# A graph network on one core: the second convolution's sums as four 32-column products side by side on TensorE, and 84 gathered groups in place of 100

## The reference

```python
def _gcn_conv(x, src, dst, norm, W, b, n_nodes):
    h = x @ W
    msg = h[src] * norm[:, None]
    out = jax.ops.segment_sum(msg, dst, num_segments=n_nodes)
    return out + b
...
h = jax.nn.relu(_gcn_conv(x, src, dst, norm, W1, b1, n))
h = jax.nn.relu(_gcn_conv(h, src, dst, norm, W2, b2, n))
h = jax.nn.relu(_gcn_conv(h, src, dst, norm, W3, b3, n))
```

## Time and profile before

| | |
|---|---|
| three runs | 4913.61, 4919.73 (median), 4924.95 us |
| profiled execution | 4911.34 us, span 4909.4 us |
| TensorE matmuls busy | 4040.7 us, 82% of the span |
| VectorE, GpSimd, ScalarE busy | 3578.3, 3521.5, 2696.6 us |
| mean granted TensorE clock | 0.868 of full speed |
| convolution 2 (3091.71 to 4181 us) | 1089 us |

### The profile page before, as it was taken

The page is one execution under the profiler, slowest core; times in us unless marked ns, Lnnn a source line. Parts: engine busy times, 40 slices in busy tenths (PEclk is TensorE's granted clock), DMA queues, the critical chain, the costliest instruction groups (busy, mean ns, idle before and its releaser), DMA issues.

```text
span 4909.4 us, 169450 instructions
## 1 busy us (share of the span) xinstructions
PE 4040.7 (82%) x62463; PEld 3028.1 (62%) x62464; DVE 3578.3 (73%) x8469; ACT 2696.6 (55%) x6550; POOL 3521.5 (72%) x3660
## 2 busy tenths in 40 slices
PE   4988888888888888657666666999999999877777
PEld 2655555555555555445555555888888888455555
DVE  8999999999999999967777777344444444566666
ACT  4555555555555555477777775555555554544443
POOL 6777777777777777377777775677777774477775
PEclk9999999999999999755555555999999999767676
DMA  3111111111111122433333334333333332445454
GB/s 99 40 41 39 39 39 41 39 39 39 41 40 39 39 40 41 47 84 97 90 90 90 90 91 112 106 107 102 107 108 107 106 109 79 138 144 150 143 148 122
DMA packets 494908, 400.37 MB, mean 82 GB/s; under 512 B 269575, under 2 KB 454828, under 8 KB 493537
## 3 DMA queue, kind: packets, MB, share of 16 engines
q10 hardware_dynamic: 146996, 207.67, 12.5%
q0 software_dynamic: 115712, 109.02, 11.9%
q1 hardware_dynamic: 231536, 74.48, 7.0%
HBM read 375.52 MB, written 15.29 MB: 80 GB/s over the span
## 4 chain that ended last, share of the span: by engine, by line
POOL 56%; issue 19%; PE 19%; DVE 3%; ACT 1%; DMA 1%; POOLq 1%; DVEq 0%; SPq 0%; ACTq 0%
POOL rows L767 56%; PE radial L2050 7%; PE psT L2065 4%; PE psX L2065 3%; PE sums L2136 3%; PE radial L2192 1%; DMA rows<-table,idx 0%; PE radial L2205 0%; ACT accT L933 0%; DVE scratch L1116 0%; DMA xn<-in_x 0%; PE radial L1991 0%; DVE rows L1810 0%; PE radial L2004 0%; DMA table<-arena 0%
## 5 line engine op out<-in xcount | busy, mean ns | idle before, releaser
L767 POOL DMA_INDIRECT rows<-table,idx x3616 | 3495.0, 967 | 1266.9 <-issue 1155.9
L2050 PE MATMUL radial<-arena,shared 128*32 128x96 bf16 (+1 forms) x31200 | 917.2, 264 | 179.2 <-DVE shared L1596 73.5
L1925 PEld LDWEIGHTS sums<-scratch,onehot 128*64 128x64 f32 x9408 | 794.9, 136 | 397.5 <-DVE scratch L1360 228.7
L1925 PE MATMUL sums<-scratch,onehot 128*64 128x264 f32 (+1 forms) x9408 | 925.0, 340 | 70.0 <-DVE scratch L1360 58.3
L2050 PEld LDWEIGHTS radial<-arena,shared 128*32 128x32 bf16 (+1 forms) x31200 | 657.0, 114 | 315.9 <-issue 77.7
L1343 DVE TENSOR_TENSOR scratch<-radial,shared 128x768 f32<-128x768 f32 x784 | 740.7, 945 | 0.0
L990 ACT CAST scratch<-radial 128x480 bf16<-128x480 f32 x860 | 476.4, 554 | 455.5 <-PE radial L2050 432.7
L833 ACT ACTIVATE dist<-iota,rel 128x64 f32<-128x64 f32 (+1 forms) x2368 | 619.4, 343 | 45.2 <-issue 24.1
L1910 PE MATMUL radial<-shared 64*128 64x384 f32 x3136 | 639.0, 484 | 0.0
L863 ACT COPY shared<-rows 128x192 f32<-128x192 f32 x196 | 88.9, 453 | 838.9 <-DMA rows<-table,idx 828.7
L1335 DVE TENSOR_TENSOR scratch<-radial,shared 128x512 f32<-128x512 f32 x784 | 533.1, 680 | 13.3 <-issue 13.3
(11 more groups left out here) (236 smaller groups left out, 5458.3 us busy)
## 6 DMA issues: line engine op xcount, KB each, us to landing
scratch<-places_d ACTq DMA_DIRECT2D x242, 800.0 KB
rows<-table,idx POOLq DMA_INDIRECT x3616
shared<-in_edge_weight SPq DMA_DIRECT2D x390, 128.0 KB, 2.8
idx<-in_src SPq DMA_DIRECT2D x451, 4.0 KB
table<-arena SPq DMA_DIRECT2D x24, 256.0 KB, 2.4
table<-arena SPq DMA_DIRECT2D x2, 1176.0 KB, 10.6
accT<-in_edge_attr SPq DMA_DIRECT2D x2, 1152.0 KB
table<-arena SPq DMA_DIRECT2D x24, 96.0 KB, 2.0
```

Of the source, the lines that this page charges most:

```text
L767: (pool.indirect_dma_start(rows_3[:, r, j, :] if n in (1, 3) else rows[:, r, j, 0:WIDTH[n]], None, tables[n], bass.IndirectOffsetOnAxis(ap ...
L1925: last = nc.tensor.matmul(there, onehot[:, u % 2, 4 * h + t, 0:SW], taken_from, start=(h + q + part == 0), stop=(h == 1 and q == 1 and par ...
L2050: last = nc.tensor.matmul(d, from_src[n][:, h, i, t, :], table_of(n, s), start=True, stop=True, tile_position=(0, 32 * i))
```

## The change

The change does four things, all in convolution 2.

1. `give` takes the products the other way round. Weights are now strips of 32 features of `taken` (128x32), moving are the 96 columns of destination marks; four strips go to four positions of the array. The result is 128 features x 96 nodes, as in `accT`. Five products become twenty, written in the source.
2. `gathered_sum` is split in the same way: four strips of 32 features of the gathered rows as weights, 80 columns of marks moving. Eight products become 32.
3. `copy_given` and `turn_given` are gone, and `add_bucket` reads `psT` or `psX` directly, one chunk earlier in VectorE's order.
4. Gathered groups go from 100 to 84 and buckets from 70 to 82 (410 chunks), in seven passes in place of eight.

```diff
-GATHERED = [NG, 92, 100, 64]
-LOOP = [(UNROLL, 0), (12, 10), (12, 8), (8, 12)]
-REST = [(UNROLL, 0), (8, 6), (16, 14), (8, 12)]
+GATHERED = [NG, 92, 84, 64]
+LOOP = [(UNROLL, 0), (12, 10), (12, 12), (8, 12)]
+REST = [(UNROLL, 0), (8, 6), (12, 10), (8, 12)]
...
-            def copy_given(step, v):
...
             def add_bucket(n, step, v_, u):
...
-                if n == 2:
-                    dve.wait_ge(given_turned, given_count(step, v_))
-                    sums_of = (psX if v_ % 2 else psT)[:, HID:HID + BWIN]
-                else:
-                    dve.wait_ge(bucket_summed, chunk_count(n, step, v_ * NCK + NCK - 1))
-                    sums_of = (psX if v_ % 2 else psT)[0:rows_, 0:BWIN]
+                dve.wait_ge(bucket_summed, chunk_count(n, step, v_ * NCK + NCK - 1))
+                sums_of = (psX if v_ % 2 else psT)[0:rows_, 0:BWIN]
...
-                        if k % NCK == (2 if n == 2 else 1) and not (first and k < NCK):
+                        if k % NCK == 1 and not (first and k < NCK):
                             add_bucket(n, step, k // NCK - 1, u)
...
+            feature_tiles = [slice(i * F, (i + 1) * F) for i in range(4)]
+
             def give(n, step, k):
...
                     if n == 2:
-                        last = nc.tensor.matmul((psX if v % 2 else psT)[0:BWIN, 0:HID], to_dst[n][:, h, t, :], taken[n][:, h, t, :],
-                                                start=(c + t == 0), stop=(c * KC + t == KB - 1))
+                        for f in feature_tiles:
+                            last = nc.tensor.matmul((psX if v % 2 else psT)[f, 0:BWIN], taken[n][:, h, t, f], to_dst[n][:, h, t, :],
+                                                    start=(c + t == 0), stop=(c * KC + t == KB - 1), tile_position=(0, f.start))
...
-            def turn_given(step, v):
...
-                        mm = nc.tensor.matmul(sums[0:w, u % 2, 0:CWIN], far_rows[j],
-                                              (onehot if n == 2 else onehot_3)[0:counts[j], u % 2, j, 0:CWIN],
-                                              start=(j == 0), stop=(j == max(i for i in range(TPG) if counts[i])))
+                        marks = (onehot if n == 2 else onehot_3)[0:counts[j], u % 2, j, 0:CWIN]
+                        for f in feature_tiles if n == 2 else [slice(0, w)]:
+                            mm = nc.tensor.matmul(sums[f, u % 2, 0:CWIN], far_rows[j][:, f], marks, start=(j == 0),
+                                                  stop=(j == max(i for i in range(TPG) if counts[i])),
+                                                  tile_position=(0, f.start))
```

More of the change, by code:

```diff
@@ L223, in gnn_kernel @@
             "p (h t f) -> p h t f", h=2, t=KC)
-        given = scratch[0:BWIN, NB * F + 2 * KB * CAP + 2 * KC * HID:2 * NB * F].rearrange("p (h f) -> p h f", h=2)
         ident_h = shared[:, 5456:5456 + P // 2].bitcast(bf16)
@@ L418, in gnn_kernel @@
         bucket_added = sem("bucket_added")
-        given_copied = prefix_copied
-        given_turned = prefix_made
         odd_counted = sem("odd_counted")
@@ L470, in bucket_count @@
             return step.times(LOOP[n][1], sum(BUCKETED[:n]) + v + 1 + plus)
-        def given_count(step, v, plus=0):
-            return step.times(LOOP[2][1], NBG + v + 1 + plus)
         def chunk_count(n, step, k, plus=0):
@@ L1027, in body @@
                         v, c = divmod(k, NCK)
-                        if n == 2 and c == 0 and not (first and v == 0):
-                            copy_given(step, v - 1)
                         for i, part in parts:
@@ L1040, in body @@
                         store_places(step, RANKS_LAST - 1, last)
-                    if last and n == 2:
-                        copy_given(step, chunks_ // NCK - 1)
                 if n == 1:
@@ L1744, in body @@
                             dve.wait_ge(*when(added, step, u - 1, before=rounds_before(n)))
-                            v_done = (k - (8 if n == 2 else 7)) // NCK
+                            v_done = (k - 7) // NCK
                             if not no_chunk(n, step, v_done * NCK):
@@ L2070, in give @@
                 last.then_inc(bucket_summed, 1)
-            def turn_given(step, v):
-                pe.wait_ge(given_copied, given_count(step, v))
-                nc.tensor.transpose((psX if v % 2 else psT)[:, HID:HID + BWIN], given[:, v % 2, :],
-                                    ident[0:BWIN, 0:BWIN]).then_inc(given_turned, 1)
             def odd_edges(n):
@@ L2152, in body @@
                             give(n, step, k - 1)
-                        if n == 2 and k % NCK == 1 and not (first and k == 1):
-                            turn_given(step, k // NCK - 1)
                         if n == 1 and k > 0:
@@ L2163, in body @@
                         give(n, step, chunks_ - 1)
-                    if last and n == 2:
-                        turn_given(step, chunks_ // NCK - 1)
                     if last and n == 1:
```

## The result

The changed kernel takes 5142.7 us (median of four runs, 5140.7 to 5146.4) against 4919.0 of the kernel before beside it: ratio 1.0455, 95% interval 1.0437 to 1.0473. Slower, as forecast, 43 us above the forecast 5100.

What follows compares the result with a forecast made beforehand. It took TensorE's instruction feed to bound changed convolution 2: 317 packets x 4.0 us = 1268 us, 179 more than now; 4911.3 + 179 = 5090, and with the runs' median 8.4 above, 5100 us, range 4830 to 5420.

Steps and rivals of the forecast that it cites:

- TensorE bounds the stage, before and after: In convolution 2, TensorE alone accounted for the present 1089 us; GpSimd, VectorE and ScalarE would stay hidden under it.
- The number of packets: Instruction fetches for TensorE in convolution 2: 317 blocks of 256 instructions after the change, where the trace before has 177.
- Time of a packet, 4.0 us: Spacing of TensorE's instruction fetches in convolution 2: 4.0 us taken, between 3.6 and 4.7, giving a stage of 1268 us.
- The stretch of 3.36 us without a stop: After a stop at 4673.03, TensorE ran 117 products in 3.36 us; read as the quickest fetch of 256 instructions.
- the break-even rival: Instruction fetches every 3.4 to 3.5 us everywhere in convolution 2: stage 1078 to 1110 us, total 4910 to 4940; chance 0.05.
- Array work, 1010 us: TensorE's products in convolution 2: 410 chunks at 2.15, 84 groups at 1.23 and 26 us for jumps; bounds 918 and 1200.
- my lower bound of 918: TensorE's products in convolution 2 would take 918 us if the joins between the two shapes went.
- the array sets the pace: Instruction feed keeps up in convolution 2: stage 1010 us, total 4840, or 4750 with no joins; faster, chance 0.20.
- The sum: Convolution 2 as 317 instruction fetches of 4.0 us: 1268 us, 179 more than now.
- The rule of the Trainium skill: The sequencer fetches the next 256 instructions while executing the current ones, mostly hidden; convolution 2 would then take 1010 us.
- The rival of a stage at 0.72: In convolution 2 TensorE's granted clock falls to a mean of 0.72: stage 1450 us, total 5280; chance 0.10.
- What was to be seen: In convolution 2: 100 or more "issue" stops within runs of products, 317 or more packets, mean chunk near 2.8 us.

## Why the prediction was right, point by point

- *TensorE bounds the stage, before and after.* Right: VectorE and ScalarE wait for it in both traces; GpSimd waits 11 us for it before and 413 us after. In the changed kernel it is the feed of TensorE's instructions and no longer its array.
- *The number of packets.* 317 were counted from the built program; the stage has 323 (317 are those of the 1295 us window, which leaves some of the stage out). Right within 2%.
- *Time of a packet, 4.0 us.* Measured 4.08. The value was nearly right by a sum whose terms were wrong: I had 3.4 us as the time without a load and 1.5 us for each load; the runs show 3.85 and 0.9. By its terms the sum gave 3.8; 4.0 was picked between that and 4.15, so that it came so near is partly luck. The stretch of 3.36 us without a stop, which I took as the time of a packet, was not one. It ends before the next stop does, and the same timeline of the kernel before goes on so:

```profile
4677.19 0.52 PE L2136 MATMUL sums<-onehot,rows 128*96 128x80 bf16 x8 [0.58 <-issue]
```

  From 4673.03 to 4677.19 are 4.16 us, with 255 recorded instructions. No run of the experiments had a mean under 3.79, though single packets came quicker, such as the 3.54 us above. So nothing here bears out the break-even rival (3.4 to 3.5 everywhere).
- *Array work, 1010 us.* Too high: 410 x 1.92 + 84 x 1.10 + 26 = 906 us, near my lower bound of 918, since the joins did go. (The 26 is too high as well: the loop jumps back four times here and five times before, where I had counted six and seven.) `give` costs 0.83 us and not 0.92, `take` 1.09 and not 1.23 (starts at 3329.20, 3330.29 and 3331.12 in its timeline). It cost the forecast nothing, as the array doesn't set the pace; had the rival "the array sets the pace" come true, it would have been about 4740.
- *The sum.* Stage 1268 forecast, 1319.6 measured. Of the 52 us that are short, six more packets make 24, 0.08 us more for each packet makes 25, and the rest is the last `give` behind the last `take`. The total came out 43 us above the forecast.
- *The rule of the Trainium skill.* The Trainium skill, "Runtime: NRT & Kernel Launch", section "Instruction fetch mechanics", calls a crossing of a block mostly hidden. The trace disagrees here: 295 us of matmul idle with "issue" as its end. Where 256 instructions take the array longer than 3.8 us, as in the kernel before and with two strips, it agrees.
- *The clock.* 0.96 over the window 3200 to 4200, against 0.99. The rival of a stage at 0.72 didn't come; what came was short spells at long stops (below).
- *What was to be seen.* Stops in the midst of runs with "issue", and GpSimd waiting for `gathered_sum`: both there. The mean chunk, about 2.8 us forecast, is (1320 - 84 x 1.10 - 26)/410 = 2.9 with the stops of the groups in it. The step prices between stops came out lower than forecast: 1.09, 0.83 and 1.10 us.

## What to carry to other kernels

Count a tiled product's instructions beside its columns. Here 256 TensorE instructions took 3.8 us or more in the mean of every run, 14.8 ns each: four strips want one each 11 ns (1.92 us for some 173) and starve, two strips each 17 ns (2.21 us for 133) and run at the array's pace. Before a step is cut finer, look in the trace for stops in the middle of a run with no semaphore, and measure from one to the next; and when work is shifted between two methods, shift it toward the one that is cheap in what is scarce, here in instructions.

## What the runs showed of the hardware that was not expected

A packet's time depends little on what else moves: 4.09 us at 88 GB/s with 800 KB loads, 3.85 with the loads cut to 32 KB, 3.80 at 16 GB/s. The trace of the changed kernel takes it apart in part. Between 3095 and 4300 us, 195 times one packet's worth of instructions (215 to 260 recorded) lies between two stops, and each time exactly one packet falls between them: in the median its transfer begins 1.39 us after TensorE has gone on and takes 1.04 us, and TensorE goes on 1.40 us after the transfer's end. With small loads and gathers it is 1.34, 0.99 and 1.40. So here the next packet is fetched only once TensorE works on the one before, and a stop ends when it has come. What fills the 1.4 us on either side is open.

At many long stops the clock falls for a few microseconds. The stage of the changed kernel has 23 spells of the lower level (0.5 of full speed, 1.2 GHz), 106 us in all; each begins within a stop of 2 us or more or at most 1.4 us behind one, while 14 of the 37 such stops have none, one of 3.54 us among them. The stretch 3642.6 to 3646.2 of the changed kernel follows a stop of 2.26 us, and its row shows a granted clock of 0.62; in the stretch 3648.4 to 3652.2 it is back at 1.00:

```profile
3642.60:3646.20 3.60, 3.60 (x100) 3.60 (x104) 1.54 (x3) 1.18 (x3) 2.22 (x3) 0.62 0.09 24
3648.40:3652.20 3.80, 3.80 (x169) 3.80 (x162) 2.43 (x5) 1.47 (x5) 3.09 (x3) 1.00 0.21 57
```

So a mean of 0.96 is 2.4 GHz with spells of the lower level. In the slow spell 204 instructions take 3.6 us, so the next packet can be in time, which is how I read that no stop follows at once.

Strips of 32 columns side by side with `take` also of that shape save the joins; two strips of 64 keep them: `take` is 1.23 us from start to start there, 1.09 with four.
